# Selective scan with top-k experts on one core: B with time on partitions by three transposes of copied rows in place of 24 narrow matmuls, and the copy of rows ahead of the second softplus

## The reference, cut to what matters

```python
# 1. attention inside segments: every second token of segments of 256, three segments of 128 rows
probs = softmax(einsum('bsqd,bskd->bsqk', x, x) / 16); h = einsum('bsqk,bskd->bsqd', probs, x)
# 2. selective scan (state size 16, inner width 512) on layernorm(h), added to h
x_in, z = split(norm(h) @ W_in.T, 2)
u = silu(causal_conv4(x_in) + b_conv)
dt = softplus(u @ W_dt.T + b_dt)
Bm = u @ W_B.T          # 384 times x 16 states
Cm = u @ W_C.T
h_t = exp(dt_t * A) * h_(t-1) + dt_t * Bm_t * u_t        # for each of the 16 states
y_t = sum over states of h_t * Cm_t
h = h + (y * silu(z)) @ W_out.T
# 3. 8 of 64 experts by grouped top-k, at most 256 tokens each, added to h
```

## Time and profile before

| | |
|---|---|
| runs | 3737.77 us median of 3 (3730.68 to 3738.78) |
| the profiled execution | 3755.1 us, its span 3752.9 us |
| mean granted TensorE clock in it | 0.950 of full speed |
| first scan to last scan | 87.7 to 3205.1 us |
| counting and experts | behind 3205.1 us |

### The profile page before, as it was taken

How to read it: one execution, slowest core, us unless ns; L and a number is a source line. 1 busy time by engine, 2 the same in 40 slices (tenths; PEclk the granted TensorE clock), 3 DMA queues, 4 the chain that set the end, 5 groups by cost and what they waited for, 6 DMA issues and landing times. The chain is left out here.

```text
span 3752.9 us, 63833 instructions
## 1 busy us (share of the span) xinstructions
PE 3115.0 (83%) x19681; PEld 2513.8 (67%) x19681; DVE 2904.9 (77%) x4755; ACT 2874.3 (77%) x5580; POOL 2106.4 (56%) x780
## 2 busy tenths in 40 slices
PE   5889888888888888888888888888888887566664
PEld 3777777677777777777777777677677777544543
DVE  2777888888888888888888888888888888544442
ACT  4989899888889888988898889888888888121110
POOL 0655555555555555555555555555555557157776
PEclk9999999999999999999999999999999999678897
DMA  2111111111111111111111111111111111167775
GB/s 85 40 40 54 58 57 58 58 49 58 57 36 57 58 58 58 58 58 54 53 58 58 58 54 45 58 58 58 50 58 45 49 52 51 43 139 150 148 151 87
DMA packets 175718, 241.44 MB, mean 64 GB/s; under 512 B 32816, under 2 KB 154128, under 8 KB 175376
## 3 DMA queue, kind: packets, MB, share of 16 engines
q1 hardware_dynamic: 150800, 199.44, 16.6%
q0 software_dynamic: 24576, 37.77, 6.1%
HBM read 176.07 MB, written 61.08 MB: 63 GB/s over the span
## 5 line engine op out<-in xcount | busy, mean ns | idle before, releaser
L349 POOL TENSOR_TENSOR hid<-hid,c_all 128x1536 f32<-128x1536 f32 x512 | 1771.1, 3459 | 1437.4 <-DVEq L561 1434.2
L566 DVE TENSOR_TENSOR_SCAN hid<-decay,hid,psB 128x1024 f32<-128x1024 f32 x512 | 1201.6, 2347 | 171.5 <-PE psB L830 131.2
L367 ACT ACTIVATE dbu_t<-dtu_t,b_t 128x512 f32<-128x512 f32 x1536 | 995.0, 712 | 275.9 <-PE psB L830 275.4
L830 PE MATMUL psB<-ident,dbu_t 128*128 128x128 f32 x6144 | 884.5, 281 | 309.0 <-DVE hid L566 295.7
L379 ACT ACTIVATE decay<-dt,a_neg 128x383 f32<-128x383 f32 x2048 | 1086.4, 606 | 0.0
L830 PEld LDWEIGHTS psB<-ident,dbu_t 128*128 128x128 f32 x6144 | 701.4, 144 | 463.6 <-DVE hid L566 389.2
L842 PE MATMUL psY<-ident,hid 128*128 128x128 f32 x6144 | 788.3, 280 | 3.5 <-POOL hid L349 3.5
L566 DVE TENSOR_TENSOR_SCAN hid<-decay,psB 128x512 f32<-128x512 f32 x512 | 624.1, 1219 | 186.9 <-PE psB L830 161.6
L842 PEld LDWEIGHTS psY<-ident,hid 128*128 128x128 f32 x6144 | 718.6, 146 | 3.7 <-POOL hid L349 3.7
L902 PE MATMUL psM<-u,w_dt 128*128 128x384 f32 x1024 | 352.0, 487 | 3.8 <-ACT soft L413 2.0
L902 PEld LDWEIGHTS psM<-u,w_dt 128*128 128x128 f32 x1024 | 184.6, 190 | 106.9 <-ACT soft L413 3.2
(11 more groups left out here) (148 smaller groups left out, 3544.9 us busy)
## 6 DMA issues: line engine op xcount, KB each, us to landing
c_all<-bc_rows_dram SPq DMA_DIRECT2D x128, 768.0 KB, 4.8
out_dram<-h SPq DMA_DIRECT2D x64, 384.0 KB, 4.0
h<-out_dram SPq DMA_DIRECT2D x32, 384.0 KB, 3.4
x_weights_dram<-normed SPq DMA_DIRECT2D x32, 384.0 KB, 2.4
xs<-in_x_dram SPq DMA_DIRECT2D x32, 256.0 KB
e_wg<-in_gate_dram SPq DMA_DIRECT2D x64, 128.0 KB
e_wu<-in_up_dram SPq DMA_DIRECT2D x64, 128.0 KB
e_wd<-in_down_dram SPq DMA_DIRECT2D x64, 128.0 KB
```

Of the source, the lines that this page charges most:

```text
L349: nc.gpsimd.tensor_tensor(hid[k % 4][:, :, :], hid[k % 4][:, :, :], c_all[:, k, :].unsqueeze(1).to_broadcast([P, CH, L]), ALU.mult).then_i ...
L367: last = nc.scalar.activation(dbu_t[k % 2][:, t, :], dtu_t[q][:, t, :], ACT.Copy, scale=b_t[q][:, t, k:k + 1])
L566: nc.vector.tensor_tensor_scan(h[:, lo:hi], flat(decay[k % 4])[:, lo:hi], flat(psB)[:, lo:hi], h[:, lo - 1:lo] if j else 0.0, ALU.mult, AL ...
L830: last = nc.tensor.transpose(flat(psB)[:, i * P:(i + 1) * P], dbu_t[k % 2][:, t, c * P:(c + 1) * P], ident[:, :])
```

## The change

TensorE no longer computes B a second time at step 9. ScalarE's copy bc_rows gets 128 partitions, cleared once, of which 32 are written; at step 14 TensorE turns its three blocks of 128 times (turn_b) into a new product BT, in slot 1 between YT2 and O1, and ScalarE copies the first 16 columns of each block into b_t (copy_b). On ScalarE the second softplus goes behind copy_prob_t in step 8. The scaling of the next sequence waits for BT where it waited for CB.

```diff
--- before.py
+++ after.py
@@ -52,7 +52,7 @@
 LATE = ("X2T0", "X2T1", "LG")
 
 SLOTTED = (("XN0", "X0", "X2", "Z0", "Z2", "D0", "D1", "D2", "X2T0", "D3", "X2T1", "AT0", "YT0", "DU0", "DU2", "O0"),
-           ("XN1", "X1", "X3", "Z1", "QT0", "QT1", "S", "PT", "CB", "AT1", "YT1", "DU1", "YT2", "O1", "LG"))
+           ("XN1", "X1", "X3", "Z1", "QT0", "QT1", "S", "PT", "CB", "AT1", "YT1", "DU1", "YT2", "BT", "O1", "LG"))
 
 
 def sequence_phase(nc, x, w, bc_dram, h_out, x_tab, ch_tab):
@@ -100,7 +100,7 @@
         soft = sb("soft", [P, CH, L])
         yz_t = sb("yz_t", [P, NSEG, DI])
         yz = sb("yz", [P, CH, L])
-        bc_rows = sb("bc_rows", [2 * NS, L])
+        bc_rows = sb("bc_rows", [P, L])
         c_all = sb("c_all", [P, NS, L])
         decay = [sb(f"decay{j}", [P, CH, L]) for j in range(4)]
         hid = [sb(f"hid{j}", [P, CH, L]) for j in range(4)]
@@ -273,7 +273,7 @@
             def store_bc(n, b, r):
 
                 wait(s_out[slot("CB")], number("CB", b))
-                sp.dma_start(bc_dram[r], bc_rows[:, :]).then_inc(s_bcw, 16)
+                sp.dma_start(bc_dram[r], bc_rows[0:2 * NS, :]).then_inc(s_bcw, 16)
                 wait(s_bcw, 16 * (n + 1))
 
             def share_c(b, r, g):
@@ -361,7 +361,7 @@
                 s = NS * b + k
                 if k == 0:
                     act.wait_ge(s_out[slot("DU2")], number("DU2", b - 1))
-                    act.wait_ge(s_out[slot("CB")], number("CB", b - 1))
+                    act.wait_ge(s_out[slot("BT")], number("BT", b - 1))
                 after(act, s_bt, PB * (s - 1))
                 for t in range(NSEG):
                     last = nc.scalar.activation(dbu_t[k % 2][:, t, :], dtu_t[q][:, t, :], ACT.Copy,
@@ -423,10 +423,13 @@
             def copy_bc(n, b, r):
                 filled("CB", b)
                 after(act, s_bcw, 16 * n)
-                nc.scalar.activation(b_t[r][:, :, :].rearrange("p t n -> p (t n)"),
-                                     psM[slot("CB")][:, L:L + NSEG * NS], ACT.Copy)
-                nc.scalar.activation(bc_rows[:, :], psM[slot("CB")][0:2 * NS, 0:L],
+                nc.scalar.activation(bc_rows[0:2 * NS, :], psM[slot("CB")][0:2 * NS, 0:L],
                                      ACT.Copy).then_inc(s_out[slot("CB")], 1)
+
+            def copy_b(b, r):
+                filled("BT", b)
+                nc.scalar.activation(b_t[r][:, :, :], psM[slot("BT")][:, 0:L].rearrange(
+                    "p (t n) -> p t n", t=NSEG)[:, :, 0:NS], ACT.Copy).then_inc(s_out[slot("BT")], 1)
 
             def probs(a):
                 act.wait_ge(s_nm, a + 1)
@@ -486,6 +489,8 @@
                         first_rstd(o, 1)
                     if early and k == 13:
                         first_rstd(a, 0)
+                    if front and k == 14:
+                        copy_b(b, r)
                     if of:
                         scaled_dbu(*of)
                     if front:
@@ -501,8 +506,6 @@
                             act.preload_act_table_set("natural_log_exp_and_others")
                         if k in (5, 6, 7, 8):
                             biased_dt(b, k - 5)
-                        if k == 8:
-                            softplus(n, b, 1)
                         if k == 12:
                             copy_dtu(b, r, 0)
                             copy_dtu(b, r, 1)
@@ -521,6 +524,8 @@
                         softplus(n, b, 0)
                     if early and k == 8:
                         copy_prob_t(b)
+                    if front and k == 8:
+                        softplus(n, b, 1)
                     if front and k == 9:
                         copy_bc(n, b, r)
                     if back:
@@ -546,6 +551,7 @@
             for j in range(4):
                 nc.vector.memset(decay[j][:, :, 0:1], 0.0)
             nc.vector.memset(xin[:, :, 0:TAPS - 1], 0.0)
+            nc.vector.memset(bc_rows[:, :], 0.0)
             nc.vector.memset(epsc[:, :], EPS)
             nc.vector.memset(xs[:, NSEG - 1, :], 0.0).then_inc(s_const, 1)
 
@@ -907,12 +913,17 @@
                 emptied("CB", b)
                 to = psM[slot("CB")]
                 for k in range(CH):
-                    nc.tensor.matmul(to[0:2 * NS, 0:L], w_bc[:, k, :], u[:, k, :], start=(k == 0), stop=(k == CH - 1))
+                    last = nc.tensor.matmul(to[0:2 * NS, 0:L], w_bc[:, k, :], u[:, k, :], start=(k == 0),
+                                            stop=(k == CH - 1))
+                last.then_inc(s_in[slot("CB")], 1)
+
+            def turn_b(b):
+                copied("CB", b)
+                emptied("BT", b)
                 for t in range(NSEG):
-                    for k in range(CH):
-                        last = nc.tensor.matmul(to[:, L + t * NS:L + (t + 1) * NS], u[:, k, t * P:(t + 1) * P],
-                                                w_bc[:, k, 0:NS], start=(k == 0), stop=(k == CH - 1))
-                last.then_inc(s_in[slot("CB")], 1)
+                    last = nc.tensor.transpose(psM[slot("BT")][:, t * P:(t + 1) * P],
+                                               bc_rows[:, t * P:(t + 1) * P], ident[:, :])
+                last.then_inc(s_in[slot("BT")], 1)
 
             def turn_dtu(n, b, t):
                 if t == 0:
@@ -1007,6 +1018,8 @@
                             turn_dtu(n, b, 1)
                         if k == 13:
                             turn_dtu(n, b, 2)
+                        if k == 14:
+                            turn_b(b)
                     if back:
                         if k == 11:
                             turn_yz(m, b, 0)
```

## The result

| | before | changed |
|---|---|---|
| runs | 3738.28 us median of 4 (3730.68 to 3743.93) | 3613.91 us median of 4 (3612.05 to 3617.02) |
| ratio | | 0.9669, 95% interval 0.9651 to 0.9688 |
| profiled execution, its span | 3755.1 us, 3752.9 | 3613.6 us, 3611.7 |
| first scan to last scan | 87.7 to 3205.1 us | 83.0 to 3066.7 us |
| a sequence without a slow stretch of the clock | 96.92 us | 93.54 us |

A forecast was written before the change was run, and what follows sets the result against it. The prediction took VectorE's scans as the bound, waiting at step 10 for TensorE's L830 behind step 9's products. Terms -103.9 (31 sequences at -3.35), -4 and -22 gave -130 us, so 3608 us, range 3582 to 3643.

The forecast's parts named there:

- The narrow passes: Step 9: removing TensorE's 24 passes of 16 columns ahead of L830 takes 2.70 us off each sequence.
- The softplus: Step 8: the second softplus behind the copy of the probabilities lets L910 start earlier, 0.98 us less a sequence.
- The three transposes: Step 14, ahead of the output projection: three transposes add 0.33 us a sequence, without waits for YT2 or the slot.
- The slower rival: Output projection waits for the slot until ScalarE copies B; at 6 us late, 3766 us in all; chance 0.04.
- Ahead of the first scan: Before the first sequence: removed passes and swap shorten a chain with nothing beside it, 4 us less once.
- The clock: Step 10, second scan: 14 stretches at 1.2 GHz, 1.6 us each, go; 22 us less, bounds 0 and 45.
- The others stay as they are: Other slow clock stretches, behind the routing matmul at the loop's turn, were expected to stay unchanged.
- The rule on transposes: Skill's rule that the full clock does not engage for transposes; trading 24 counted passes for three would add slow stretches.
- ScalarE as the pace: Steps 10 to 15: transposes wait for ScalarE, so a sequence gains only 1.7 us; 3659 us, chance 0.08.
- Slow stretches at every step 10: Step 10: a slow clock stretch in every sequence, 27 us more in place of 22 less; 3657 us, chance 0.05.
- The copy of B as the wait: Step 14 to 15: TensorE may not write O1 before ScalarE copies BT; 3766 us, chance 0.04.
- Hidden passes: Step 9: the removed passes were hidden anyway and VectorE finds an equally long wait; 3738 us, chance 0.02.

The follow-up runs named there:

- the four hidden copies: Changed kernel with four extra 128x384 ScalarE copies ahead of the copy of B at step 14; 3622.0 us, ratio 0.9683 to the kernel before.
- the wide ones: Changed kernel with the 24 passes put back at 128 moving columns instead of 16, results unused; 3707.1 us, ratio 0.9882 to the kernel before.
- the fastest version: Changed kernel with B turned at step 10 beside the attention in its bank, copied ahead of step 11's scaled dbu; 3603.7 us, ratio 0.9635.

## Why the prediction was right

**The path.** The forecast rested on one chain of step 9, and each link moved as worked out. The narrow passes: 2.70 us forecast, 2.73 measured alone and 2.68 when put back. The softplus: 0.98 forecast, 1.01 measured, in 30 sequences and not in 31 (1 us in all). The scan of step 10 was to start with the other two conditions met just before: VectorE's idle time is 0.56 us, forecast at 0.6 or less.

**The three transposes.** 0.33 us forecast, 0.32 measured; no wait for YT2 (0.1 us of spare was forecast, some 0.4 is there) and none for the copy of B. Here the working was too careful in one place: the slack at the slot was 2.15 us and not 1.8. The slower rival needed 5.2 us of lateness to lose against the kernel before; when made, 3.3 us of lateness cost 1.31 of the 3.38 gained.

**Sum for a sequence**: 3.35 forecast, 3.38 measured. Ahead of the first scan 4 forecast, 4.6 measured (3.7 in the second pair of profiles). This makes 31 x 3.38 + 4.6 = 109 us, forecast 108; less the swap that the last sequence does not have, 108.

**The clock** is the only term with an error to speak of. 22 us were forecast, the medians leave 124 - 109 = 15 on the first chip and 131 - 109 = 22 on the second; the two profiled executions, which lie 141 us apart, some 30 of it. The stretches of 1.6 us at step 10 are all gone, in both profiles of the changed kernel. (They were 15 and not 14: of every second sequence from 9 on, sequence 13 has none, and sequence 30 has one.) "The others stay as they are" was the weak step. Their number stayed (15 in the profile before, 15 after), but they moved: at the loop's turn 9 before and 3 after, at step 11 4 before and 11 after. In most sequences with one of the latter step 14 takes 0.5 to 0.6 us longer (6.19 in place of 5.61); one at the turn costs the first step of the next sequence 1.4 us (9.30 in place of 7.88). For the two profiled executions this splits the 30 us, as sums over the 31 sequences beyond the undisturbed step lengths: some 25 for steps 9 and 10, where 22 were forecast, some 11 at the loop's turn, and 4 lost at step 14. The last two were put at nothing, and in this pair they make 7 us; so that the medians come out so near the forecast 22 is in part luck. The medians can't be split so: the spread between executions of the kernel before (18 us on one chip) is as large as what is left.

**The stated range** does not follow from its own terms at the lower end: 3585 less the 12 us for the sequences' terms is 3573, and 3582 was given (the upper end, 3630 + 12, is right). The result lies far from either.

**The rule on transposes.** By the Trainium skill (TensorE: Matmul & The Clock Gate, Part 4) transposes don't count towards the full clock. The changed kernel is against it as the earlier trace rows were: TensorE did nothing but transposes from 1460 to 1470.5 us, at a granted clock of 1.00 (window below), and with fewer true passes the kernel as a whole has fewer slow stretches, not more. That transposes hold the clock as well as other passes do is not shown: each of the 11 slow stretches at step 11 began 5.6 to 6.9 us after the attention of step 10, the last passes that are not transposes, with a standstill of at least 2.05 us in between. The same stretch of work in sequence 14 kept the full clock.

```profile
97.00:2990.00 2893.00, 2571.12 (x17010) 2071.75 (x17009) 2586.41 (x3735) 2676.57 (x5043) 1709.36 (x495) 0.99 0.18 57
1460.00:1470.50 10.50, 8.69 (x75) 7.87 (x74) 9.93 (x14) 10.47 (x22) 8.10 (x3) 1.00 0.35 127
```

**The rivals.** ScalarE as the pace: refuted by a sequence that is 3.38 us shorter, where this rival gave 1.7, and at step 14 by the four hidden copies. Slow stretches at every step 10: none there. The copy of B as the wait: real, but beyond 2 us. Hidden passes: refuted by the 87 us of the wide ones.

## What to carry to other kernels

Cost an engine in order by what stands ahead of the instruction that the bounding engine waits for, and check the other conditions of that wait: here three were met within 0.6 us of each other once the path was shorter, and 3.7 of the 4.25 us came back. Before an instruction is put into an idle hole, look at who filled its buffer last, not only at who needs it next: with B turned at step 11, behind a product filled just before, the kernel lost over 60 us; with B turned one step earlier and copied at once, the hole of 2 us at step 11 hid the wait and each sequence gained 0.33 us. Work that nobody waits for is free in its own engine and still not free if it holds back a slot for longer than the slack.

## What the runs showed of the hardware

- A float32 pass of 128x128 weights takes 0.113 us start to start with 16 moving columns and 0.116 with 128, both at the full clock.
- The same 24 passes at the same place are followed by the 1.2 GHz clock in 15 of 31 sequences when 16 columns move, in none when 128 do: 24 us between two kernels whose undisturbed sequences are equally long. Narrow passes alone do not bring it: the fastest version has six of 16 columns at step 10 and no slow stretch there.
- A wait of TensorE can cost twice, and a short one in the middle of a hole can pay. With its longest standstill at step 11 at 3.75, 2.70, 2.06 and 0.84 us, the clock fell there in 26, 17, 11 and none of the 31 sequences. The second and the last differ in the place of one copy of 0.2 us, and by 49 us (measured on two chips; 39 by their ratios to the kernel before).
